# Decoder layer: bulk loads and stores in a few large transfers, the cross-attention stage as one stream of 128 steps, and five unused products ahead of it

## What is computed

```
x = x + linear_attention(layernorm(x))           # no softmax; q, k normalised per head
q, k, v = feature_map(layernorm(x)), feature_map(ctx), feature_map(ctx)
          # per head: z = x_head @ fm_w.T + fm_b ; concat(exp(z), exp(-z)) -> 16 features
scores = einsum('nqhd,nkhd->nhqk', q, k) / sqrt(128)
attn   = softmax(scores, axis=-1)                 # over 77 keys, 16 heads, 32 sequences
x = x + einsum('nhql,nlhd->nqhd', attn, v).reshape(32, 128, 256) @ fc_w.T + fc_b
x = x + ffn(layernorm(x))                         # shared expert + 16 routed experts, top 1
```

## Time and profile before

| | |
|---|---|
| device time, 3 runs | 653.83 to 665.1 us, median 655.98 us |
| the profiled execution | 653.2 us, span 651.4 us |
| mean granted TensorE clock | 0.866 of full speed |
| phase 1 | 0 to 131.7 us of the span |
| phase 2 | to 199.8 us (first product of phase 3) |
| phase 3 | to 424.9 us |
| phase 4 | to 651.4 us |

### The profile page before, as it was taken

The page is one execution under the profiler, slowest core; times in us unless marked ns, Lnnn a source line. Parts: engine busy times, 40 slices in busy tenths (PEclk is TensorE's granted clock), DMA queues, the critical chain, the costliest instruction groups (busy, mean ns, idle before and its releaser), DMA issues.

```text
span 651.4 us, 11782 instructions
## 1 busy us (share of the span) xinstructions
PE 464.6 (71%) x3778; PEld 316.6 (49%) x3778; DVE 341.8 (52%) x969; ACT 253.6 (39%) x578; POOL 190.8 (29%) x223
## 2 busy tenths in 40 slices
PE   0488898677731298888889888868982198887760
PEld 0266566444421166566566665524551155766650
DVE  4577885427686246666665666475820123434343
ACT  0446655377750034444443444536710012323320
POOL 3142231657882000000000000020077400555550
PEclk9999999878885559988985889969997599989995
DMA  5720000016689979999997890000041001566739
GB/s 98 282 95 1 0 0 2 0 42 195 198 144 174 181 89 112 117 105 113 104 112 75 90 97 3 3 1 1 1 145 52 33 0 45 157 194 188 203 95 258
DMA packets 101485, 61.94 MB, mean 95 GB/s; under 512 B 33832, under 2 KB 99656, under 8 KB 101320
## 3 DMA queue, kind: packets, MB, share of 16 engines
q1 hardware_dynamic: 91976, 52.92, 46.7%
q0 software_dynamic: 2560, 5.31, 2.4%
q10 hardware_dynamic: 6912, 3.25, 2.2%
HBM read 40.34 MB, written 20.73 MB: 94 GB/s over the span
## 4 chain that ended last, share of the span: by engine, by line
PE 40%; DVE 15%; SPq 12%; issue 8%; DMA 7%; ACT 7%; another core or an unknown queue 7%; POOL 1%; ACTq 1%; DVEq 0%; POOLq 0%
SPq L473 5%; PE bank L711 4%; PE bank L696 4%; PE bank L1204 3%; DMA kst<-kparts 2%; PE bank L1215 2%; ACT prob L853 2%; PE bank L1214 2%; SPq L629 2%; DMA qst<-mT 2%; PE bank L1263 2%; PE bank L734 2%; PE bank L740 2%; PE bank L666 2%
## 5 line engine op out<-in xcount | busy, mean ns | idle before, releaser
L853 ACT ACTIVATE prob<-bank 77x512 f32<-77x512 f32 x128 | 73.7, 592 | 109.7 <-PE bank L696 109.1
L870 POOL COPY vcur<-vals 77x272 f32 (+1 forms) x32 | 13.2, 416 | 190.5 <-PE bank L711 190.5
L1178 POOL DMA_INDIRECT routed<-t_y,t_no x48 | 45.9, 956 | 75.1 <-DVE t_y L1047 63.9
L778 DVE TENSOR_REDUCE mx<-bank 128x5 f32<-128x385 f32 (+1 forms) x96 | 53.7, 580 | 25.1 <-PE bank L666 23.3
L711 PE MATMUL bank<-prob,vcur 77*17 77x128 f32 x1024 | 57.4, 300 | 12.7 <-ACT prob L853 12.4
L666 PE MATMUL bank<-kst,qst 96*128 96x77 bf16 x512 | 40.7, 224 | 34.2 <-DMA kst<-kparts 28.9
L696 PE MATMUL bank<-qst,kst 99*77 99x128 bf16 x512 | 57.4, 243 | 6.7 <-DMA qst<-mT 6.7
L696 PEld LDWEIGHTS bank<-qst,kst 99*77 99x77 bf16 x512 | 43.8, 132 | 17.1 <-issue 9.4
L825 DVE COPY avs_s<-bank 128x512 f32<-128x512 f32 x32 | 22.1, 692 | 56.7 <-PE bank L711 56.7
L666 PEld LDWEIGHTS bank<-kst,qst 96*128 96x128 bf16 x512 | 31.7, 114 | 37.3 <-DMA kst<-kparts 15.5
L941 DVE TENSOR_TENSOR act<-bank,s_g 128x512 f32<-128x512 f32 x24 | 16.5, 688 | 63.3 <-ACT s_g L1115 49.9
(11 more groups left out here) (178 smaller groups left out, 1071.7 us busy)
## 6 DMA issues: line engine op xcount, KB each, us to landing
qst<-qparts SPq DMA_DIRECT2D x96, 128.0 KB, 5.3
t_w<-in_expert_w SPq DMA_DIRECT2D x48, 192.0 KB
qparts<-qpart SPq DMA_DIRECT2D x16, 384.0 KB, 3.4
kparts<-kpart SPq DMA_DIRECT2D x48, 77.0 KB
kst<-kparts SPq DMA_DIRECT2D x16, 231.0 KB, 7.8
sorted_in<-fill SPq DMA_DIRECT2D x1, 3168.0 KB, 10.4
t_row<-sorted_in ACTq DMA_DIRECT2D x48, 66.0 KB
kst<-kparts SPq DMA_DIRECT2D x16, 154.0 KB, 8.1
```

What stands on the lines that cost most here:

```text
L778: v.tensor_reduce(mx[:, n // 3, h0:h1], bank[n % 2][:, 0:(h1 - h0) * KEYS].rearrange("p (h k) -> p h k", k=KEYS), AX.X, ALU.max).then_inc( ...
L853: a.activation(prob[u % 2][:].rearrange("p c t -> p (c t)"), bank[2 + u % 2][0:KEYS], ACT.Exp, scale=SCORE_SCALE).then_inc(s["expd"], 1)
L1178: p.indirect_dma_start(out=routed, out_offset=bass.IndirectOffsetOnAxis(ap=t_no[r][:].bitcast(U32), axis=0), in_=t_y[r][:], in_offset=None ...
```

## The change

- The parts in memory get another layout, group of four sequences first, then part, feature, head, token. The map's columns are reordered (feature first, then head) so that a store is one transfer for all three parts: for k two stores for each phase-2 group instead of six.
- Loads go by groups of four sequences: three for q and three for k, in rows that are contiguous for all heads (16 KB for q, 9.6 KB for k), the repeated q parts by a broadcast source. `NBUF` falls to 3; the third buffer lies where phase 2 has its tiles. The groups 0 and 1 are loaded within phase 2, the group 2 after its last store.
- Phase 3 has no hardware loop. It is a list of 128 steps (32 sequences x 4). The product with the values runs two steps behind the shifted scores (`LAG = 2`), with three `prob` buffers and two banks for its result; the scores run four sequences ahead. The tail is spread over two sequences.
- The 512-wide copy of the result goes from VectorE to ScalarE. The negation goes into the maxima. GpSimd no longer copies values, adds the bias one sequence at a time, and issues the shift's small transfers, which SyncE's queue did.
- Ahead of step 0 and behind the scores of the first four sequences TensorE runs five products of 128 x 256 whose result nobody reads.

The core of the diff:

```diff
-        qparts = nc.dram_tensor("qparts", (HEADS, EX, PARTS, TOK), BF16).ap()
-        kparts = nc.dram_tensor("kparts", (PARTS, EX, HEADS, B * KEYS), BF16).ap()
+        qparts = nc.dram_tensor("qparts", (NG, PARTS, EX, HEADS, GT), BF16).ap()
+        kparts = nc.dram_tensor("kparts", (NG, PARTS, EX, HEADS, JK), BF16).ap()
...
-                    for a in range(PARTS):
-                        sp.dma_start(kparts[a, :, heads, bass.ds(g * JK, JK)].rearrange("e h t -> h e t"),
-                                     kpart[par][hf][:, a]).then_inc(k_sent[par][hf], 16)
+                    sp.dma_start(kparts[g, :, hf * HD:(hf + 1) * HD].rearrange("a e h t -> (e h) a t"),
+                                 kpart[par][hf][:]).then_inc(k_sent[par][hf], 16)
...
+                if g == 2:
+                    sent(0, 1)
+                    load_q(sp, 0)
+                if g == 3:
+                    load_k(sp, 0)
+                if g == 5:
+                    sent(1, 2)
+                    load_q(sp, 1)
+                if g == 6:
+                    load_k(sp, 1)
...
+        def load_q(sp, group):
+            r = group % NBUF
             for at, part, n in Q_RUNS:
-                for i in range(n):
-                    sp.dma_start(qst[r][(at + i) * EX:(at + i + 1) * EX],
-                                 qparts[:, :, part, bass.ds(g * JA * S, JA * S)].rearrange("h e t -> e h t")).then_inc(parts_in[r], 16)
+                same = qparts[group, part].rearrange("e (o h) t -> e o h t", o=1).broadcast_to([EX, n, HEADS, GT])
+                sp.dma_start(qst[r][at * EX:(at + n) * EX], same).then_inc(parts_in[r], 16)
+        def load_k(sp, group):
+            r = group % NBUF
             for at, part, n in K_RUNS:
                 sp.dma_start(kst[r][at * EX:(at + n) * EX],
-                             kparts[part:part + n, :, :, bass.ds(g * JA * KEYS, JA * KEYS)].rearrange("a e h t -> (a e) h t")).then_inc(parts_in[r], 16)
+                             kparts[group, part:part + n].rearrange("a e h t -> e a h t")).then_inc(parts_in[r], 16)
...
+            all_sent(sp, NG // 2)
+            sp.wait_ge(s["vp"], NG)
+            load_q(sp, 2)
+            load_k(sp, 2)
+            for group in range(3, NG):
+                sp.wait_ge(s["bp"], (group - 2) * (2 * 4 * JA))
+                load_q(sp, group)
+                load_k(sp, group)
...
+            for b in range(JP):
+                for u in range(len(UNITS)):
+                    scores(b, u)
+                if b == 2:
+                    turn_shift(0)
+            for _ in range(5):
+                pe.matmul(bank[AV_BANK[0]][:, 0:2 * P], ident[:], fcw[:].rearrange("p k f -> p (k f)"), start=True, stop=True)
+            for n in range(STEPS):
+                b, u = n // 4, n % 4
+                shifted(n)
+                if n >= LAG:
+                    attend(n - LAG)
+                if u < len(UNITS) and b + JP < B:
+                    scores(b + JP, u)
+                if u == 0 and b % JA == 0 and b // JA + 1 < NA:
+                    turn_shift(b // JA + 1)
+                if u == 1 and b >= 2:
+                    turn_back(b - 2)
+                if u == 2 and b >= 2:
+                    project(b - 2)
+                if u == 3 and b >= 1:
+                    turn_values(b - 1)
...
+            copy_shift(0)
+            for n in range(STEPS):
+                b, u = n // 4, n % 4
+                exponentials(n)
+                if u == 0 and b % JA == 0 and b // JA + 1 < NA:
+                    copy_shift(b // JA + 1)
+                if u == 1 and b >= 1:
+                    copy_values(b - 1)
+                if u == 1 and b >= 2:
+                    copy_back(b - 2)
...
+            p.wait_ge(s["xn2"], NG)
+            for b in range(JA):
+                add_bias(b)
+            shift(0)
+            all_sent(p, NG // 2)
+            p.wait_ge(s["vp"], NG)
+            p.wait_ge(s["xb2"], JA)
+            p.memset(kst[NBUF - 1][ROWS:SHIFT_ROWS], 1.0).then_inc(s["ones_rows"], 1)
```

More of the change, by code:

```diff
@@ L43, in decoder_layer @@
     NA = B // JA
-    NBUF = 4
+    NBUF = 3
     RING = 8
@@ L761, in pe_phase3, with shifted @@
-            pe.wait_ge(s["ones_rows"], 1 + NBUF)
+            def shifted(n):
+                b, u = n // 4, n % 4
+                g = b // JA
+                r, t = home(g, b % JA)
+                if u == 0 and b % JA == 0:
+                    if g == 2 * (NBUF - 1):
+                        pe.wait_ge(s["ones_rows"], 1 + NBUF)
+                    pe.wait_ge(m_in[r], shifts(g))
+                if n >= 2:
+                    pe.wait_ge(s["expd"], n - 1)
+                for c in range(4):
+                    h = 4 * u + c
+                    i = pe.matmul(bank[2 + n % 2][0:KEYS, c * S:(c + 1) * S],
+                                  kst[r][0:SHIFT_ROWS, h, t * KEYS:(t + 1) * KEYS],
+                                  qst[r][0:SHIFT_ROWS, h, t * S:(t + 1) * S], start=True, stop=True)
+                i.then_inc(s["bp"], 1)
@@ new lines, in pe_phase3, with maxima @@
+            for n in range(STEPS - LAG, STEPS):
+                attend(n)
+            turn_back(B - 2)
+            project(B - 2)
+            turn_values(B - 1)
+            turn_back(B - 1)
+            project(B - 1)
+        def dve_phase3(v):
+            def maxima(b, u):
+                h0, h1 = UNITS[u]
+                n = b * len(UNITS) + u
+                v.wait_ge(s["ap"], n + 1)
+                v.tensor_reduce(mx[:, b % JA, h0:h1], bank[n % 2][:, 0:(h1 - h0) * KEYS].rearrange("p (h k) -> p h k", k=KEYS),
+                                AX.X, ALU.max, negate=True).then_inc(s["amax"], 1)
@@ new lines, in add_attention, with statistics @@
+            def add_attention(b):
+                v.wait_ge(s["xb2"], b + 1)
+                v.wait_ge(s["fcp"], b + 1)
+                v.tensor_tensor(xs[:, b], bank[7][:, FC], xs[:, b], ALU.add).then_inc(s["x2"], 1)
+            def statistics(b):
+                v.bn_stats(stats3[:, b], xs[:, b]).then_inc(s["stat3"], 1)
+            v.wait_ge(s["ones_rows"], 1)
+            for b in range(JP):
+                for u in range(len(UNITS)):
+                    maxima(b, u)
+                if b % JA == JA - 1:
+                    parts(b // JA)
@@ new lines, in dve_phase3 @@
+            for b in range(B):
+                for u in range(len(UNITS)):
+                    if b + JP < B:
+                        maxima(b + JP, u)
+                if b >= 2:
+                    add_attention(b - 2)
+                if b >= 1:
+                    divide(b - 1)
+                if b >= 2:
+                    statistics(b - 2)
+                if b % JA == JA - 1 and b + JP < B:
+                    parts((b + JP) // JA)
+            add_attention(B - 2)
+            divide(B - 1)
@@ L1335, in _ @@
             sp_fill(sp)
[L1336 removed]
+            sp_phase2(sp)
             sp_phase3(sp)
```

385 lines of the change are left out of this document (144 added, 241 removed).

## The result

The changed kernel takes 684.91 us (median of 4, 682.67 to 694.05), the kernel before 655.84 beside it: 1.044 times the time, 95% interval 1.040 to 1.049. The prediction was 597. (Some executions of one and the same kernel are some per cent slower, at a lower granted clock: medians here are of all executions, ratios with an interval leave the slow ones out.) The profiled execution took 682.67 us, its span is 680.9, its mean granted clock 0.808 (before 0.866).

The account below looks back on a forecast made before the run. At full clock TensorE's order and waits bound phase 3, transfers close behind. Start 203.5 + 31.75 x 4.85 + 3 + 6.9 puts phase 4 at 367.4, 57.5 us earlier: 597 us, forecast range 580 to 611, 580 to 632 with rivals.

Parts of the forecast that it names:

- I take the fast end, so transfers leave the chain: Phase 3 loads: 2.52 MB a group lands in 6.5 us at 388 GB/s, within 19.4 us, so the 8.79 us wait goes.
- I bound by 2 us and by 3.8 us: Start of phase 3: landing time of the first shift's small transfers, putting step 0 between 201.8 and 203.6 us.
- I cost both at nothing: Phase 2: fewer, merged k stores and two added loads cost nothing; 0 to 8 us if a load holds the stores.
- ScalarE waiting for stores: Phase 2: sign named in advance that the predicted start of phase 3 is wrong.
- I take 3 us: Stream of phase 3: total loss to half clock, about 8 us of sequences at 7.7 us instead of 4.85.
- Rival 3: Stream: clock stays low, 7.7 to 8 us a sequence, phase 4 at 458, 686 us in all; chance 0.07.
- Period: Stream of phase 3: time for one sequence, 4.65 to 5.3 us, taken as 4.85.
- Step 0 at 203.5: Start of phase 3: the first shifted scores begin at 203.5 us, when the five unused products end at half clock.
- Products: Ahead of step 0: five unused TensorE products run from 199.2 to 203.5 us, 4.3 us at half clock.
- rival 1: Stream: waits between engines stay, 5.4 to 6.0 us a sequence, 620 us (612 to 630); chance 0.14.
- the prediction's list of waits: Stream: exponential and division waits gone, maxima 0 to 0.4 us, new ScalarE copy about 0.15; 0.2 us placed a sequence.
- Last shifted scores to phase 4 and the sum: End of stream: step 127 at 360.5 us plus an unchanged 6.9 us chain, so phase 4 starts at 367.4, not 424.9.

Follow-up runs that it names:

- e9: Changed kernel with q's three large loads issued behind one landed shift and k's three behind the next; 674.7 us, 1.008 of the kernel before.
- e4: Changed kernel with the shift's two transfers issued by ScalarE's queue behind its own copy instead of by GpSimd; 714.7 us, 1.094 of the kernel before.
- e5: Changed kernel with a 64-byte gap behind each head, so rows of 1 KB and 616 bytes, and nine loads a group; 697.6 us, 1.057 of the kernel before.
- e16: Changed kernel with a group's six large loads each issued two steps after the one before; 612.3 us, 0.991 of the kernel before.
- e10: Changed kernel with every load cut to head 0 and all scores formed from it, other heads left out; 597.2 us, 0.896 of the kernel before.
- e6: Changed kernel with only the phase 2 loads of groups 0 and 1 cut to head 0; 672.0 us, 1.010 of the kernel before.
- e7: e3 plus one unused product ahead of each turn of the maxima (15); 622.7 us, 0.936 of the kernel before.
- e13: e7 plus 31 unused products, one behind each turn of the values; 573.2 us, 0.943 of the kernel before.
- e3: Changed kernel with each load cut into four transfers of four heads, 24 small ones a group; 632.3 us, 0.956 of the kernel before.
- e1: Changed kernel with each bulk load from group 2 on held until the same step's shift has landed; 671.4 us, kernel before 656.8 beside it.

## Why the prediction was wrong

**The step that failed: "I take the fast end, so transfers leave the chain".** The 6.5 us for 2.52 MB came from a window at 388 GB/s. In the changed kernel a load takes 18.5 us (issued from 251.1 on, landed at 269.6), nearly three times that; in e9, where q's and k's parts go apart, q's last piece lands 11.8 us after its issue and k's last 6.8. Longer rows didn't bring the fast rate: from 252 to 268 us the DMA share is 0.93 at 159 GB/s. Why isn't shown. The load still lands in time, with 19.4 us to do it in, and the step asked for no more than that: it did not ask what the load does to a small transfer behind it.

**The landing of the shift, "I bound by 2 us and by 3.8 us".** The 2 us are right where nothing is ahead (2.1 us is the shortest in nearly every run). 3.8 us was the landing beside *today's* loads, pieces of 77 to 231 KB, each group of two sequences by itself. Six issues of 154 to 768 KB put the whole load ahead of the shift at once: 12 to 13 us, the first 8 of them before its first packet. e4 excludes the queue, e5 the rows, e9 and e16 show the backlog, e10 its absence. The Trainium skill, DMA: Bandwidth & Descriptors, Queues, rings and completion order, says that each DMA engine changes between the queue rows that have work after every packet. By that rule a shift in a queue of its own should come up after one packet of the load on each engine. In the changed kernel 138 packets of the load, some 9 on each of 16 engines, pass before its first, and in e5, with short rows, 1267 (258.9 to 269.4 us), some 79 on each. If a packet of the trace is one of the page's, the runs speak against the rule; whether it is one isn't shown.

**Phase 2, "I cost both at nothing".** The bound of 0 to 8 us for the two loads was too small: 14 us (e6). ScalarE waits 11.9 us for stores of k, which land after 10.6 instead of 2.9 us. It is the same mechanism as the shift. The prediction had named the right watch, ScalarE waiting for stores, and priced the cover ("some 14 us") without asking how long a store takes beside a load.

**The clock, "I take 3 us".** Measured 50 us. The term counted one slow start; it left out that the stream falls back to half clock behind its stands, and that a long landing makes stands just at full clock. Rival 3 had the price (686 us, measured 684.9) and the chance of 0.07. That the two agree so well is luck: it priced all 32 sequences at half clock, 18 were, and the late start and the waits made up the rest. Its reason, that this mix may not hold the full clock, is refuted by e10; what raised its chance was a wait, and the prediction had held that wait to be gone. The Trainium skill, TensorE: Matmul & The Clock Gate, Part 1, says that sustained activity releases the clock. 71.5 us busy of 73 at 0.50 in the changed kernel don't fit that; nor did.

**What held.** Period: 4.85 predicted, 5.07 measured, inside 4.65 to 5.3; the last sequences, without scores, take 4.2, which makes 4.90 in the mean of e10. Step 0 at 203.5: 204.5 in e10. Products: 199.2 to 203.5 predicted, 4.3 us; 4.62 measured, at half clock. Waits between engines (rival 1): only VectorE's parts, 0.9 us in every second sequence, which the prediction's list of waits left out. Phase 4: 226 us. Last shifted scores to phase 4 and the sum: 367.4 predicted, 367.5 in e10. So the sum was right within its terms for a kernel whose loads disturb nothing. That it meets 367.5 to 0.1 us is luck: in e10 the start is 1.0 us later, the stream 1.6 and the end 0.5 longer, and the 3 us for the clock aren't lost.

**Where the 87.5 us went** (454.9 - 367.4): 14 us in phase 2's stores; 8 us at step 0, from the shift (22.3 together); 14.5 us of later waits for shifts; 50 us of half clock. That is 87. The 50 us are priced from the periods, and that they hang on the loads is shown by e10; what made the clock fall in each stretch isn't.

## What to carry to other kernels

A large transfer is cheap by itself and dear to whatever small transfer is issued while it is queued: before merging loads, look for the small transfers on the critical path that share the DMA engines, and price them at the duration of the load ahead. Cut the load into pieces and spread their issue over the steps that it has, so that never the whole load is ahead; here that took the longest landing from 13.3 to 7.2 us. And where the clock falls after a stand, the slow stretch behind it is part of the price: in e7 some 30 us at half clock behind one wait of 1.4 us, in which e13 gained 11 us by not losing the clock.

## What the runs showed of the hardware

- A 12 KB transfer landed in 2.1 us with free DMA engines and in 12 to 13 (at most 16.3) behind a load of 2.5 MB in another queue, GpSimd's and ScalarE's alike, with rows of 16 KB and of 1 KB alike. Its first packet came 8 us after the issue, 1.2 us with free engines.
- The clock stayed at 1.00 for 155 us with 9% idle in small gaps (e10). It was at .50 for 73 us with 2% idle and no stand of note (changed kernel). The drop at 224 us of e7 came behind a wait of 1.4 us, and the rise at 405 us of the changed kernel in the middle of dense work. A wait of that length is no rule: in e3 the clock falls at 368 behind a wait of 1.20 us for VectorE's parts, with no transfer near, as the two windows show, while e10 has such a wait without a fall; e1 falls at 402 in the same way, behind 1.19 us. What decides there stays open.

```profile
364.00:368.00 4.00, 2.80 (x46) 1.95 (x39) 2.44 (x10) 1.88 (x4) 0.00 (x0) 1.00 0.00 0
368.00:402.00 34.00, 31.72 (x253) 20.99 (x253) 6.27 (x23) 15.13 (x28) 2.16 (x5) 0.51 0.01 2
```
